# Three-stage transformer kernel: in the middle stage, probabilities turned by a transposing DMA per head and scores made in 64-row tiles

## The chip, the cores and the metric

The kernel runs on one core of a Trainium2 chip. The metric is the device time of one launch in microseconds; lower is better. Engines are named as the profile names them: PE is the matrix engine (PEld its weight loads), DVE the vector engine, ACT the scalar engine, POOL the GpSimd engine, SP the engine that only issues DMAs here. SBUF is the on-chip memory that all of them read; PSUM is the small accumulator memory that PE writes, in eight banks.

## The reference

`x` is [16, 112, 256] (16 batches of 112 tokens) and the context `ctx` is [16, 375, 256]. Three blocks follow one another: a cross-attention with 16 heads of 16 and a mixture of experts (first stage), a second cross-attention with 16 heads of 64 over context and tokens together (middle stage), and a mixture of 8 experts (last stage). The change touches the middle one:

```
heads, dim_head = (16, 64)
xn = layer_norm(x, g1, b1)                   # here x is the context, 375 rows
ln_lat = layer_norm(latents, g2, b2)         # 112 rows
q = ln_lat @ Wq
kv = jnp.concatenate([xn, ln_lat], axis=1) @ Wkv     # 375 + 112 = 487 rows
...
weight = jnp.einsum('bhld,bhnd->bhln', q * scale, k * scale)     # 112 x 487 a head
weight = jnp.where(full_mask[:, None, None, :], weight, neg)
weight = jax.nn.softmax(weight.astype(jnp.float32), axis=-1).astype(q.dtype)
out = jnp.einsum('bhln,bhnd->bhld', weight, v)
out = out.transpose(0, 2, 1, 3).reshape(b, l, heads * dim_head)
return out @ Wout
```

## The kernel before

Everything is computed in near float32 precision with 16-bit matmuls. A number is split into a high half (its float16 rounding) and a low half (what is left), and a product is three matmuls: high by high, high by low, low by high (`PASSES`).

The kernel has three stages, one after the other, each with its own program for each engine. The middle one is `phase_attention_large_heads`. Its names start with `b_` in the profile. It goes over the 16 batches. The bodies of batches 2 to 13 are a hardware loop of two batches an iteration (`run_batches`), the others are written out. A batch's body is 16 steps `s`, one a head (H = 16). There is no scheduler: each engine runs a list in the order of the code and waits on counters (`need`).

Work of a batch, by the steps of the body:

- **Projections** (`item`, 18 a batch, steps in `PSLOT`), for the batch after: 8 of K (128 x 487 results, 6 matmuls each), 2 of Q (24 matmuls of 112 columns), 8 of V (122 x 512 results, 6 matmuls; the 487 keys are cut in 4 blocks of KB1 = 122). Each result goes through one of two PSUM banks `ps_p`: ACT writes the high half, DVE the low half.
- **Stacking** (`stack`, on SP): a head has only 64 rows of K and Q, so DMAs put the high and low halves of K on top of one another (`k_stack`, 4 DMAs of 487 KB) and double those of Q (`q_dup`, 8 of 112 KB). This makes one head's three products two matmuls over 128 rows (`scores`).
- **Softmax**: `maxima` on DVE reads the scores from PSUM with the mask (`keep`) and writes `prob` and the row maxima; `exps` on ACT takes the exponential in place and the sums. `prob` is a ring of 4 heads (`RING`).
- **Transposes**: the product with V needs the probabilities with keys as rows. PE transposes `prob` in float32, 4 transposes a head, into a PSUM bank `ps_t` (`transposes`, two steps behind the scores). ACT copies out the high half (`phi`) and DVE the low half (`plo`), into `pT`, a ring of 2.
- **Values** (`values`, three steps behind the scores): 12 matmuls of 64 columns a head into one of two banks `ps_o`. `out_heads` on DVE divides by the sums once a batch.
- **Small work** (`XSLOT`, on a lent bank, `ps_x = ps_o[1]`): output projection, norms and the router for the batch before (`hitem`), transposes of the tokens two batches ahead (`nitem`). POOL splits tokens, makes the mask bias and rows for the experts, and splits the experts' weights for the last stage in chunks (`split_chunk`, 384 KB loads and stores).

Inside a step PE's list is: scores of head s, transposes of head s - 2, projections of the next batch, values of head s - 3, small work.

Of the kernel before, what the change touches and what calls it, by code (L numbers as in the profile page):

```python
# [16 lines left out]
ALU = mybir.AluOpType  # L17
# [8 lines left out]
B = 16  # L26
# [957 lines left out]
KB1, NB1 = 122, 4  # L984
# [3 lines left out]
def phase_attention_large_heads(nc, ctx_tok, mask, g_xattn, g_ffn, g1, b1, g2, b2, wr, br, consts, w_s,  # L988
# [6 lines left out]
    with ExitStack() as ctx:  # L995
# [32 lines left out]
        q_s = sb("q_s", [128, 2, IT, T], F16)  # L1028
        q_dup = [sb(f"q_dup{i}", [128, 2, H, T], F16) for i in range(2)]
        k_s = sb("k_s", [128, 2, IT, NK], F16)  # L1030
        k_stack = [sb(f"k_stack{i}", [128, H, NK], F16) for i in range(2)]
# [7 lines left out]
        pT = sb("pT", [128, 2, 2, NB1, 128], F16)  # L1039
# [67 lines left out]
        s_kstack = sem("kstack")  # L1107
        s_qdup = sem("qdup")
# [3 lines left out]
        s_tr = sem("tr")  # L1112
        s_phi = sem("phi")
        s_plo = sem("plo")
# [45 lines left out]
        XSLOT = {3: ("n", 0), 4: ("h", 0), 5: ("h", 1), 6: ("n", 1), 7: ("h", 2), 8: ("n", 2), 9: ("h", 3), 10: ("h", 4)}  # L1160

        def lent_before(s):

            n = [XSLOT[t][0] for t in XSLOT if t < s]
            return n.count("h"), n.count("n")
# [8 lines left out]
        def _(sp):  # L1174
            settled = (s_zero, 8)

            def load(c):
# [3 lines left out]
                sp.dma_start(x2_t[:, :], x2_dram[c]).then_inc(s_xload, 16)  # L1181
                need(sp, s_keep, 1, c, 0, settled)
                sp.dma_start(keep_u[:, :], mask[c].partition_broadcast(T)).then_inc(s_mload, 16)

            def stack(c, par):


                need_all(sp, settled, (s_ihi, PI, c, P_Q), (s_ifree, PI, c, P_Q), (s_score, H, c - 1, 1))
                for a in range(2):
                    for part in (HI, LO):  # L1190
                        src = k_s[64 * a:64 * a + 64, part, :, :]
                        rows = part if a == 0 else 1 - part
                        sp.dma_start(k_stack[par][64 * rows:64 * rows + 64, a::2, :], src).then_inc(s_kstack, 16)
                need_all(sp, settled, (s_ihi, PI, c, P_V), (s_ifree, PI, c, P_V))
                for a in range(2):
                    for rows in range(2):
                        for part in (HI, LO):
                            sp.dma_start(q_dup[par][64 * rows:64 * rows + 64, part, a::2, :],
                                         q_s[64 * a:64 * a + 64, part, :, :]).then_inc(s_qdup, 16)
# [5 lines left out]
            def store(c):  # L1205
                need(sp, s_hfree, HI_, c, H_X + 1, settled)
                sp.dma_start(acc_dram[bass.ds(c * T, T), :], x3[:, :]).then_inc(s_store, 16)

            def body(b, par):
                if not first(b):  # L1210
                    residual(b - 1)
                if ahead(b, 2):
                    load(b + 2)
                if ahead(b, 1):
                    stack(b + 1, 1 - par)
                if not first(b):
                    store(b - 1)

            load(0)
            load(1)  # L1220
            stack(0, 0)
            run_batches(sp, body)
            residual(B - 1)
# [4 lines left out]
        def _(pool):  # L1228
# [7 lines left out]
            pool.memset(prob[:, :, NK:NKP], 0.0).then_inc(s_zero, 1)  # L1236
# [24 lines left out]
            def split_tokens(c, par):  # L1261

                for k, cols in enumerate(TOK):
                    need_all(pool, settled, (s_nfree, NI, c, k + 1), *([(s_item, PI, c - 1, 0)] if k == 0 else []))
                    if first(c):
                        pool.wait_ge(s_thi, k + 1)
                    else:
                        pool.tensor_copy(tok_s[par][(slice(None), HI) + cols], tok_f[(slice(None),) + cols]).then_inc(s_tsplit, 1)
                        need(pool, s_tsplit, 6, c, 2 * k + 1)
                    pool.tensor_tensor(tok_s[par][(slice(None), LO) + cols], tok_f[(slice(None),) + cols],  # L1270
                                       tok_s[par][(slice(None), HI) + cols], ALU.subtract).then_inc(s_tsplit, 2 if first(c) else 1)
# [31 lines left out]
            def split_chunk(b, par, j, pair):  # L1303
# [5 lines left out]
                pool.tensor_tensor(wch_s[j][:, LO, :], wch_f[j][:, :], wch_s[j][:, HI, :], ALU.subtract).then_inc(s_wch, 1)  # L1309
                need(pool, s_wch, 4, b, 2 * j + 2, settled)  # L1310
# [17 lines left out]
            def choose(c):  # L1328
# [7 lines left out]
                pool.tensor_tensor(both[:, :], chosen[:, 0, :], chosen[:, 1, :], ALU.add).then_inc(s_chosen, 1)  # L1336
                need(pool, s_meta, 5, c, 0, settled)
# [8 lines left out]
            def send_rows(c):  # L1346
# [913 lines left out]
```

## Time and profile before

| | |
|---|---|
| time, median of 3 runs | 1531.97 us (1529.74 to 1535.42) |
| profiled execution, its own time | 1528.29 us |
| its span | 1526.3 us |
| PE busy | 1357.1 us (89%) |
| DVE busy | 1177.2 us (77%) |
| ACT busy | 954.2 us (63%) |
| POOL busy | 654.9 us (43%) |
| middle stage | from about 500 to 1315 us |
| mean granted TensorE clock | 0.953 |

Busy times count overlapping instructions of one engine once. Durations of single matmuls are longer than their share of the stream, since they are pipelined; the distance from one start to the next tells what one costs.

### The profile page before, as it was taken

What the parts mean: (1) busy time and instruction counts of PE and PEld (TensorE: products, weight loads), DVE (VectorE), ACT (ScalarE), POOL (GpSimd) and SP (SyncE); (2) the same over time, 40 slices, a digit from 0 to 9 for tenths busy, and PEclk for the clock granted to TensorE, in tenths of its full rate; (3) what the DMA queues carried; (4) which work ended last, traced back from release to release, by engine and by line L of the source; (5) the groups of instructions that cost most, each with busy time, mean ns of one, the idle gap of its engine ahead of it and who ended that gap; (6) DMA issues with size and microseconds to landing.
All of it is one profiled execution on the core that took longest, in us unless ns stands there. A gap on an engine that the chain in (4) does not pass through costs nothing. (4 is left out here: it accounts for less than half of the span.)

```text
span 1526.3 us, 45153 instructions
## 1 busy us (share of the span) xinstructions
PE 1357.1 (89%) x14276; PEld 1053.6 (69%) x14276; DVE 1177.2 (77%) x3350; ACT 954.2 (63%) x2456; POOL 654.9 (43%) x1044
## 2 busy tenths in 40 slices
PE   5999999999974799999999999999999997279995
PEld 3788888888751367776776677767766776278994
DVE  4899999999863388887887877878878787267772
ACT  4887888888951366665666665656656666045663
POOL 3544444444543234342543344334534424235654
PEclk8999999999976899999999999999999999589998
DMA  5333333333201666346653565447634671473323
GB/s 163 100 117 115 115 101 115 115 111 97 72 8 34 130 135 127 88 90 129 144 110 69 120 144 108 91 94 145 125 80 96 130 160 48 136 287 55 61 40 73
DMA packets 167807, 163.36 MB, mean 107 GB/s; under 512 B 81274, under 2 KB 155394, under 8 KB 164528
## 3 DMA queue, kind: packets, MB, share of 16 engines
q1 hardware_dynamic: 151440, 118.80, 34.2%
q0 software_dynamic: 13168, 35.80, 9.3%
q10 hardware_dynamic: 3024, 6.47, 1.5%
q8 instruction: 106, 1.74, 0.5%
q14 instruction: 69, 0.57, 0.1%
HBM read 64.48 MB, written 41.96 MB: 70 GB/s over the span
## 5 line engine op out<-in xcount | busy, mean ns | idle before, releaser
L1414 PE MATMUL b_ps_p<-b_tok_s,w_s 128*128 128x112 f16 (+1 forms) x1536 | 223.3, 300 | 11.3 <-DVE b_k_s L1698 6.6
L1709 DVE CUSTOM_DVE_ANT_0 b_prob<-b_ps_s,b_keep 112x487 f32<-112x487 f32 x256 | 167.9, 656 | 27.4 <-PE b_ps_s L1493 26.3
L1414 PE MATMUL b_ps_p<-w_s,b_tok_s 128*122 128x512 f16 x768 | 186.9, 379 | 0.0
L1605 ACT ACTIVATE b_prob<-b_prob,b_top 112x487 f32<-112x487 f32 x256 | 177.6, 694 | 10.5 <-DVE b_top L1709 10.3
L1414 PEld LDWEIGHTS b_ps_p<-b_tok_s,w_s 128*128 128x128 f16 x1536 | 117.5, 100 | 95.9 <-issue 17.9
L1611 ACT ACTIVATE b_pT<-b_ps_t 122x448 f16<-122x448 f32 x256 | 137.7, 538 | 72.1 <-PE b_ps_t L1501 69.6
L1493 PE MATMUL b_ps_s<-b_k_stack,b_q_dup 128*112 128x487 f16 x512 | 153.4, 382 | 25.6 <-issue 15.9
L1714 DVE TENSOR_TENSOR b_pT<-b_ps_t,b_pT 122x448 f16<-122x448 f32 x256 | 158.6, 619 | 6.9 <-ACT b_pT L1611 5.5
L701 ACT ACTIVATE a_prob<-a_prob,a_top 112x375 f32<-112x375 f32 x256 | 156.4, 611 | 4.4 <-DVE a_top L837 3.4
L837 DVE CUSTOM_DVE_ANT_0 a_prob<-a_ps_s,a_keep 112x375 f32<-112x375 f32 x256 | 138.2, 540 | 24.4 <-PE a_ps_s L593 21.8
L1521 PEld LDWEIGHTS b_ps_o<-b_v_s,b_pT 122*128 122x128 f16 x3072 | 122.5, 98 | 44.3 <-issue 6.6
L1501 PEld LDWEIGHTS b_ps_t<-b_const,b_prob 112*122 112x122 f32 x1024 | 121.6, 140 | 37.7 <-issue 1.5
L1584 ACT ACTIVATE b_k_s<-b_ps_p 128x487 f16<-128x487 f32 x128 | 73.9, 578 | 113.6 <-PE b_ps_p L1414 113.6
L842 DVE TENSOR_TENSOR a_pT<-a_ps_t,a_pT 125x336 f16<-125x336 f32 x256 | 128.2, 501 | 18.2 <-ACT a_pT L708 12.4
L1501 PE MATMUL b_ps_t<-b_const,b_prob 112*122 112x112 f32 x1024 | 142.2, 261 | 0.0
L1521 PE MATMUL b_ps_o<-b_v_s,b_pT 122*128 122x64 f16 x3072 | 131.8, 193 | 5.4 <-DVE b_pT L1714 3.4
L602 PE MATMUL a_ps_t<-a_const,a_prob 112*125 112x112 f32 x768 | 127.8, 275 | 9.0 <-ACT a_prob L701 7.1
L602 PEld LDWEIGHTS a_ps_t<-a_const,a_prob 112*125 112x125 f32 x768 | 113.9, 189 | 31.3 <-ACT a_prob L701 22.5
L1593 ACT ACTIVATE b_v_s<-b_ps_p 122x512 f16<-122x512 f32 x128 | 76.4, 597 | 93.8 <-PE b_ps_p L1414 93.8
L593 PE MATMUL a_ps_s<-a_k_stack,a_q_masked 128*112 128x375 f16 x512 | 126.4, 329 | 8.1 <-DMA a_q_masked<-a_q_s 7.6
L1414 PEld LDWEIGHTS b_ps_p<-w_s,b_tok_s 128*122 128x122 f16 x768 | 97.4, 134 | 45.2 <-DVE b_v_s L1705 2.5
L1705 DVE TENSOR_TENSOR b_v_s<-b_ps_p,b_v_s 122x512 f16<-122x512 f32 x128 | 88.5, 691 | 48.6 <-ACT b_v_s L1593 48.4
(259 smaller groups left out, 3062.1 us busy)
## 6 DMA issues: line engine op xcount, KB each, us to landing
b_k_stack<-b_k_s SPq DMA_DIRECT2D x64, 487.0 KB, 11.0
xs<-a_blank SPq DMA_DIRECT2D x14, 1032.0 KB, 4.0
b_q_dup<-b_q_s SPq DMA_DIRECT2D x128, 112.0 KB, 5.2
c_w_pool<-w_split SPq DMA_DIRECT2D x8, 1600.0 KB, 10.5
b_wch_f<-in_w_experts POOLq DMA_DIRECT2D x32, 384.0 KB, 11.8
w_split<-b_wch_s POOLq DMA_DIRECT2D x32, 384.0 KB, 7.2
a_ctx_f<-in_ctxT SPq DMA_DIRECT2D x16, 375.0 KB, 3.7
a_k_stack<-a_k_s SPq DMA_DIRECT2D x64, 93.8 KB, 2.8
```

The lines of the kernel that those rows point to most:

```text
L602: last = pe.transpose(ps_t[h % 2][0:KB0, j * T:(j + 1) * T], prob[:, h % RING, j * KB0:(j + 1) * KB0], ident[0:T, 0:T])
L701: act.activation(prob[:, h % RING, :], prob[:, h % RING, :], ACT.Exp, bias=top[:, h % RING:h % RING + 1], scale=-1.0, accum_out=sums[par][ ...
L837: dve.tensor_tensor_reduce(prob[:, h % RING, :], ps_s[h % 2][0:T, 0:C], keep[par][:, :], -SCALE0, 3e38, ALU.add, ALU.min, top[:, h % RING: ...
L842: dve.tensor_tensor(pT[0:KB0, h % RING, LO, :, 0:T], ps_t[h % 2][0:KB0, 0:NB0 * T].rearrange("p (j n) -> p j n", j=NB0), pT[0:KB0, h % RIN ...
L1414: last = pe.matmul(out, sta(a, k), mov(m, k), start=(k == 0 and n == 0), stop=(k == tiles - 1 and n == 2))
L1493: last = pe.matmul(ps_s[h % 2][0:T, 0:NK], q_dup[par][:, part, h, :], k_stack[par][:, h, :], start=(part == HI), stop=(part == LO))
L1501: last = pe.transpose(ps_t[h % 2][0:KB1, j * T:(j + 1) * T], prob[:, h % RING, j * KB1:(j + 1) * KB1], ident[0:T, 0:T])
L1521: last = pe.matmul(ps_o[h // 8][:, col:col + D1], pT[0:KB1, h % 2, a, j, :], v_s[par][0:KB1, m, j, h * D1:(h + 1) * D1], start=(h % 8 == 0 ...
L1605: act.activation(prob[:, h % RING, 0:NK], prob[:, h % RING, 0:NK], ACT.Exp, bias=top[:, h % RING:h % RING + 1], scale=-1.0, accum_out=sums ...
L1611: act.activation(pT[0:KB1, h % 2, HI, :, 0:T], ps_t[h % 2][0:KB1, 0:NB1 * T].rearrange("p (j n) -> p j n", j=NB1), ACT.Copy).then_inc(s_ph ...
L1709: dve.tensor_tensor_reduce(prob[:, h % RING, 0:NK], ps_s[h % 2][0:T, 0:NK], keep[par][:, :], -SCALE1, 3e38, ALU.add, ALU.min, top[:, h % R ...
L1714: dve.tensor_tensor(pT[0:KB1, h % 2, LO, :, 0:T], ps_t[h % 2][0:KB1, 0:NB1 * T].rearrange("p (j n) -> p j n", j=NB1), pT[0:KB1, h % 2, HI, ...
```

## The change

1. The 4 PE transposes a head, their PSUM banks `ps_t`, and `phi` and `plo` go. ACT now copies the high half of `prob` straight in SBUF, rows as they are, into `halves` (`high_half`). The low half is a subtraction SBUF to SBUF, on DVE for even heads and on POOL for odd ones (`low_half`). Then SP issues one transposing DMA a head (`turn`), which writes `pT`: 112 rows of 1024 float16 (both halves, 512 columns each) become 8 blocks of 128 x 112. `pT` and `halves` are rings of 4.
2. `stack`, `k_stack` and `q_dup` go. The scores of a pair of heads are 6 matmuls over 64 rows each, in turn on rows 0 to 63 and 64 to 127, straight from `k_s` and `q_s`, which are doubled. The scores have three PSUM banks in place of two, and small work has a bank of its own.
3. The key blocks are of 128, 128, 128 and 103 rows in place of 4 of 122 (`rows_of`).
4. The lists are laid out anew by steps: values come 5 steps behind the scores (`LAG`), scores of a pair at odd steps; `PSLOT` holds 2 projections in steps 0 and 1 and one in each of the other 14; `XSLOT` has other steps and also carries `ranks`; POOL's and SP's lists are spread over the steps; the division by the sums is done by halves.

```diff
-KB1, NB1 = 122, 4
+KB1, NB1 = 128, 4
+KLAST = NK - (NB1 - 1) * KB1
+LAG = 5
...
-        ps_s = [bank(f"ps_s{i}") for i in range(2)]
-        ps_t = [bank(f"ps_t{i}") for i in range(2)]
+        ps_s = [bank(f"ps_s{i}") for i in range(3)]
...
-        ps_x = ps_o[1]
+        ps_x = bank("ps_x")
...
-        for s, n in enumerate([2, 2, 2, 2, 1, 1, 0, 1, 1, 1, 1, 1, 1, 1, 1]):
+        for s, n in enumerate([2, 2] + [1] * 14):
...
+            def turn(b, h):
+
+                need_all(sp, settled, (s_lo[h % 2], H // 2, b, h // 2 + 1), (s_pv, H, b, h - RING + 1))
+                sp.dma_start(pT[:, h % RING, :, :, 0:T].rearrange("p s j n -> p (s j) n"),
+                             halves[:, h % RING, :, :].rearrange("p s n -> p (s n)"), transpose=True).then_inc(s_turned[h % RING], 16)
...
+            def scores(b, par, pair):
+
+                if pair == 0:
+                    need(pe, s_ihi, PI, b, P_V)
+                    need(pe, s_ifree, PI, b, P_V)
+                need(pe, s_max, H, b, max(2 * pair - 1, 0))
+                for n, (a, m) in enumerate(PASSES):
+                    for half in range(2):
+                        rows = slice(64 * half, 64 * half + 64)
+                        last = pe.matmul(ps_s[(2 * pair + half) % 3][0:T, 0:NK], q_s[par][rows, a, pair, :], k_s[par][rows, m, pair, :],
+                                         start=(n == 0), stop=(n == 2))
+                last.then_inc(s_score, 1)
...
+            def high_half(b, h):
+                need(act, s_exp, H, b, h + 1)
+                need(act, s_turned[h % RING], 16 * (H // RING), b, 16 * (h // RING))
+                act.activation(halves[:, h % RING, HI, 0:NK], prob[:, h % RING, 0:NK], ACT.Copy).then_inc(s_hi, 1)
...
+            def low_half(b, h):
+                need(dve, s_hi, H, b, h + 1)
+                dve.tensor_tensor(halves[:, h % RING, LO, 0:NK], prob[:, h % RING, 0:NK], halves[:, h % RING, HI, 0:NK],
+                                  ALU.subtract).then_inc(s_lo[0], 1)
...
             def body(b, par):
                 for s in range(H):
-                    scores(b, par, s)
-                    if not (first(b) and s < 2):
-                        c, _, h = behind(s, 2, b, par)
-                        transposes(c, h)
+                    if s == 0:
+                        scores(b, par, 0)
+                    if s % 2 == 1 and s < H - 1:
+                        scores(b, par, (s + 1) // 2)
                     if ahead(b, 1):
                         for k in PSLOT.get(s, []):
                             item(b + 1, 1 - par, k)
-                    if not (first(b) and s < 3):
-                        values(*behind(s, 3, b, par))
                     if s in XSLOT:
                         lend(b, s)
-                    if s == H - 1 and not first(b):
-                        ranks(b - 1)
+                    if not (first(b) and s < LAG):
+                        values(*behind(s, LAG, b, par))
```

On PE, late in the second batch, the list before reads (L1493 scores, L1501 transposes, L1414 a projection of V, L1521 values, L1449 small work):

```order
L1493 MATMUL b_ps_s<-b_k_stack,b_q_dup 112x487 x2
L1501 MATMUL b_ps_t<-b_const,b_prob 122x112 x4
L1414 MATMUL b_ps_p<-w_s,b_tok_s 122x512 x6
L1521 MATMUL b_ps_o<-b_v_s,b_pT 128x64 x12
L1449 MATMUL b_ps_o<-b_const,b_x_n 128x112 x2
```

and in the changed kernel, at the same place (L1537 scores of a pair, L1451 a projection of V, L1485 small work, L1552 values):

```order
L1537 MATMUL b_ps_s<-b_k_s,b_q_s 112x487 x6
L1451 MATMUL b_ps_p<-w_s,b_tok_s 128x512 x6
L1485 MATMUL b_ps_x<-b_const,b_x_n 128x112 x2
L1552 MATMUL b_ps_o<-b_v_s,b_pT 128x64 x12
L1451 MATMUL b_ps_p<-w_s,b_tok_s 128x512 x6
```

The transposes are gone, and the scores stand there every second step, as six matmuls instead of two.

On SP, the list of the second batch before is (L1203 the residual's load, L1180 to L1183 loads two batches ahead, L1207 the store):

```order
L1203 DMA b_x_res<-x 112x256
L1180 DMA b_ctx_t<-in_ctx 125x3x256
L1181 DMA b_x_t<-x 112x256
L1183 DMA b_keep_u<-in_mask 112x375
L1193 DMA b_k_stack<-b_k_s 64x8x487 x4
L1198 DMA b_q_dup<-b_q_s 64x8x112 x8
L1207 DMA acc<-b_x 112x256
```

and in the changed kernel:

```order
L1182 DMA b_ctx_t<-in_ctx 125x3x256
L1183 DMA b_x_t<-x 112x256
L1201 DMA_TRANSPOSE b_pT<-b_halves 128x8x112
L1192 DMA b_x_res<-x 112x256
L1201 DMA_TRANSPOSE b_pT<-b_halves 128x8x112 x5
L1188 DMA b_keep_u<-in_mask 112x375
L1201 DMA_TRANSPOSE b_pT<-b_halves 128x8x112 x6
L1196 DMA acc<-b_x 112x256
L1201 DMA_TRANSPOSE b_pT<-b_halves 128x8x112 x4
```

Twelve copies a batch went, and sixteen transposing DMAs came, one in each step, with the loads and the store between them.

On POOL, the list of the second batch before has its two weight chunks in a row (cast, low half, store, load of the next):

```order
L1307 CAST b_wch_s<-b_wch_f 128x768
L1309 TENSOR_TENSOR b_wch_s<-b_wch_f,b_wch_s 128x768
L1313 DMA w_split<-b_wch_s 128x2x768
L1301 DMA b_wch_f<-in_w_experts 128x768
L1307 CAST b_wch_s<-b_wch_f 128x768
```

and in the changed kernel (L1277 the low half of an odd head, L1260 the mask bias):

```order
L1314 CAST b_wch_s<-b_wch_f 128x768
L1316 TENSOR_TENSOR b_wch_s<-b_wch_f,b_wch_s 128x768
L1277 TENSOR_TENSOR b_halves<-b_prob,b_halves 112x487
L1260 TENSOR_SCALAR b_keep<-b_keep_u 112x375
L1323 DMA w_split<-b_wch_s 128x2x768
L1308 DMA b_wch_f<-in_w_experts 128x768
L1277 TENSOR_TENSOR b_halves<-b_prob,b_halves 112x487
L1314 CAST b_wch_s<-b_wch_f 128x768
```

The low half of an odd head stands behind whatever POOL does in the steps before it, a whole chunk's splitting above all.

## Rows read from the trace of the kernel before

**Rows 1.** Busy time of each engine by stretch, middle stage (last columns: clock, DMA share, GB/s).

```profile
core 0: us, PE busy (x) PEld busy (x) DVE busy (x) ACT busy (x) POOL busy (x), PEclk, DMA share, GB/s
800.00:900.00 100.00, 96.12 (x979) 70.59 (x978) 81.40 (x209) 62.15 (x142) 42.35 (x83) 0.98 0.55 114
```

**Rows 2.** The division by the sums (`out_heads`), two a batch: duration, first and last start.

```profile
L1725 DVE TENSOR_TENSOR b_o_n<-b_ps_o,b_rsum x32: 678/686/693, 584.0 to 1291.3; 112x512 f32<-112x512 f32 x32
```

**Rows 3.** Timeline of PE over one step (start us, us, what).

```profile
803.74 0.60 PE L1493 MATMUL b_ps_s<-b_k_stack,b_q_dup 128*112 128x487 f16 x2
804.18 0.55 PE L1501 MATMUL b_ps_t<-b_const,b_prob 112*122 112x112 f32 x4
804.56 1.46 PE L1414 MATMUL b_ps_p<-w_s,b_tok_s 128*122 128x512 f16 x6
805.86 0.52 PE L1521 MATMUL b_ps_o<-b_v_s,b_pT 122*128 122x64 f16 x12
806.21 0.60 PE L1493 MATMUL b_ps_s<-b_k_stack,b_q_dup 128*112 128x487 f16 x2
```

**Rows 4.** Timeline of PE where the loop starts anew, and the stretch's busy times.

```profile
716.27 1.05 PE L1493 MATMUL b_ps_s<-b_k_stack,b_q_dup 128*112 128x487 f16 x2 [2.98 <-issue]
...
716.00:718.00 2.00, 1.73 (x7) 1.33 (x8) 0.54 (x1) 0.00 (x0) 0.00 (x0) 0.53 0.21 24
```

**Rows 5.** The page's costliest groups: busy us, mean ns of one, idle before.

```profile
L1493 PE MATMUL b_ps_s<-b_k_stack,b_q_dup 128*112 128x487 f16 x512 | 153.4, 382 | 25.6 <-issue 15.9
L1611 ACT ACTIVATE b_pT<-b_ps_t 122x448 f16<-122x448 f32 x256 | 137.7, 538 | 72.1 <-PE b_ps_t L1501 69.6
L1714 DVE TENSOR_TENSOR b_pT<-b_ps_t,b_pT 122x448 f16<-122x448 f32 x256 | 158.6, 619 | 6.9 <-ACT b_pT L1611 5.5
L1584 ACT ACTIVATE b_k_s<-b_ps_p 128x487 f16<-128x487 f32 x128 | 73.9, 578 | 113.6 <-PE b_ps_p L1414 113.6
L1605 ACT ACTIVATE b_prob<-b_prob,b_top 112x487 f32<-112x487 f32 x256 | 177.6, 694 | 10.5 <-DVE b_top L1709 10.3
```

**Rows 6.** Groups of the middle stage: a low half on DVE (K) and one on POOL.

```profile
L1698 DVE TENSOR_TENSOR b_k_s<-b_ps_p,b_k_s 128x487 f16<-128x487 f32 x112 | 70.3, 658 | 26.0 <-ACT b_k_s L1584 26.0
L1309 POOL TENSOR_TENSOR b_wch_s<-b_wch_f,b_wch_s 128x768 f16<-128x768 f32 x30 | 49.4, 1645 | 4.2 <-POOL b_wch_s L1307 2.6
```

**Rows 7.** Timeline of SP's queue while a batch is stacked.

```profile
543.52 6.43 SPq L1193 DMA_DIRECT2D b_k_stack<-b_k_s  x4
550.05 11.76 SPq L1198 DMA_DIRECT2D b_q_dup<-b_q_s  x8
```

**Rows 8.** DMA queues, 540 to 560 us: share by tenths, then issues with KB and us to landing.

```profile
DMA  9590069695799999999999999999999999999999
b_k_stack<-b_k_s SPq DMA_DIRECT2D x4, 487.0 KB, 10.9
b_q_dup<-b_q_s SPq DMA_DIRECT2D x6, 112.0 KB, 5.3
b_wch_f<-in_w_experts POOLq DMA_DIRECT2D x1, 384.0 KB, 7.1
```

**Rows 9.** All 128 copies of Q: durations on SP's queue, us to landing (min/median/max).

```profile
L1198 SPq DMA_DIRECT2D b_q_dup<-b_q_s x128: 618/1774/4792, 509.3 to 1244.8; - x128
...
DMA to landing us min/median/max: 2.6/5.2/13.9
```

**Rows 10.** Timeline of PE at the first scores of the stage, and the clock there.

```profile
525.01 1.03 PE L1493 MATMUL b_ps_s<-b_k_stack,b_q_dup 128*112 128x487 f16 x2 [9.68 <-DMA b_q_dup<-b_q_s]
...
520.00:540.00 20.00, 12.34 (x55) 6.12 (x56) 10.93 (x26) 6.58 (x14) 6.50 (x9) 0.79 0.42 80
```

**Rows 11.** Timeline at the stage's end: last maxima, last values, first of the last stage.

```profile
1286.24 0.66 DVE L1709 CUSTOM_DVE_ANT_0 b_prob<-b_ps_s,b_keep 112x487 f32<-112x487 f32 x1
...
1290.12 0.51 PE L1521 MATMUL b_ps_o<-b_v_s,b_pT 122*128 122x64 f16 x12 [0.65 <-DVE b_pT L1714]
...
1315.18 0.17 PE L2035 MATMUL c_ps_a<-cum,ones 112*128 112x8 f16 x1 [7.07 <-PEq L995]
```

More of the change, by code:

```diff
@@ L1111, in phase_attention_large_heads @@
         s_exp = sem("exp")
-        s_tr = sem("tr")
-        s_phi = sem("phi")
-        s_plo = sem("plo")
+        s_hi = sem("hi")
+        s_lo = [sem("lo_even"), sem("lo_odd")]
+        s_turned = [sem(f"turned{i}") for i in range(RING)]
         s_pv = sem("pv")
@@ L1175, in _, with load_tokens @@
             settled = (s_zero, 8)
-            def load(c):
+            def load_tokens(c):
                 need(sp, s_norm, 2, c, 0, settled)
@@ L1181, in load, with load_mask @@
                 sp.dma_start(x2_t[:, :], x2_dram[c]).then_inc(s_xload, 16)
+            def load_mask(c):
                 need(sp, s_keep, 1, c, 0, settled)
                 sp.dma_start(keep_u[:, :], mask[c].partition_broadcast(T)).then_inc(s_mload, 16)
[L1185 to L1199, printed above, removed]
             def residual(c):
@@ L1497, in transposes @@
-            def transposes(b, h):
-                need(pe, s_exp, H, b, h + 1)
-                need(pe, s_plo, H, b, h - 1)
-                for j in range(NB1):
-                    last = pe.transpose(ps_t[h % 2][0:KB1, j * T:(j + 1) * T],
-                                        prob[:, h % RING, j * KB1:(j + 1) * KB1], ident[0:T, 0:T])
-                last.then_inc(s_tr, 1)
-            def values(b, par, h):
-                need(pe, s_phi, H, b, h + 1)
-                need(pe, s_plo, H, b, h + 1)
-                if h == 0:
-                    need(pe, s_oread, 2, b, 0)
+                elif kind == "n":
+                    nitem(b + 2, k)
+                else:
+                    ranks(b - 2)
@@ L1564, in _ @@
             run_batches(pe, body)
[L1565 to L1570 removed]
+            for h in range(H - LAG, H):
+                values(B - 1, 1, h)
+            need(pe, s_hfree, HI_, B - 1, 0)
+            ranks(B - 2)
+            need(pe, s_rank, 1, B - 1, 0)
             for k in range(HI_):
+                if k < H_O:
+                    need(pe, s_oread, 2, B - 1, k + 1)
                 need(pe, s_hfree, HI_, B - 1, k)
                 hitem(B - 1, k)
+            need(pe, s_hfree, HI_, B, 0)
             ranks(B - 1)
@@ L1619, in body @@
                 for s in range(H):
+                    if not (first(b) and s < 1):
+                        c, _, h = behind(s, 1, b, par)
+                        exps(c, 1 - par if s < 1 else par, h)
+                    if s == 0 and not first(b):
+                        for k in PSLOT[H - 1]:
+                            item(b, par, k)
                     if ahead(b, 1):
@@ L1653, in _ @@
             exps(B - 1, 1, H - 1)
-            phi(B - 1, H - 2)
-            phi(B - 1, H - 1)
+            high_half(B - 1, H - 1)
+            weigh(B - 2)
             for k in range(HI_):
@@ L1775, in ranks @@
                     dve.wait_ge(s_const2, NCONST2)
-                dve.tensor_tensor(rank[:, :], ps_p[0][0:T, 0:E], region[:, :], ALU.add).then_inc(s_rank, 1)
+                dve.tensor_tensor(rank[:, :], ps_x[0:T, 0:E], region[:, :], ALU.add).then_inc(s_rank, 1)
             def body(b, par):
                 for s in range(H):
+                    maxima(b, par, s)
+                    if s % 2 == 0 and not (first(b) and s < 2):
+                        c, _, h = behind(s, 2, b, par)
+                        low_half(c, h)
+                    if s == 0 and not first(b):
+                        for k in PSLOT[H - 1]:
+                            item(b, par, k)
                     if ahead(b, 1):
```

286 lines of the change are left out of this document (144 added, 142 removed).

## The prediction

> **What bounds the kernel now.** I read the busy times by stretch first: in the middle stage PE is busy 96 of 100 us, DVE 81, ACT 62, POOL 42, and the DMA engines 55% [rows 1]. The reader is to see that PE alone has no room, so this stage costs what PE's list costs. Next, the length of a batch: the divisions by the sums come twice a batch, the first starts at 584.0 us and the last, second of its pair, at 1291.3 [rows 2]. Less the 0.7 us between the two of a pair, that is 706.6 us for 15 batches, 47.1 us each. Then PE's timeline over one step, from start to start [rows 3]: two score matmuls 0.44 us, four transposes 0.38, six V matmuls 1.30, twelve value matmuls 0.35, together 2.47, with no idle time in it. The only large hole is where the loop starts anew: 2.98 us of issue, and a granted clock of 0.53 behind it, which is the 1.2 GHz level after PE had stood still [rows 4]. That comes once in two batches and belongs to the loop; I leave it in, unchanged.
>
> **The change part by part**, for a batch of 47.1 us.
>
> *The transposes go.* 16 heads by 0.38 us [rows 3]: 6.1 us off PE. Nothing lies over them, since PE is the full engine. PE: 41.0.
>
> *The scores.* Before, 16 by 0.44 = 7.0 us. Now a pair of heads takes six matmuls of 487 columns, one such being 0.22 us [rows 3]. The trace has no 64-row matmul. Below: the two halves of the array work at once, 3 by 0.22 = 0.66 us a pair. Above: they don't, 6 by 0.22 = 1.32. To either may come a drain when the array changes its shape and back. A bound for one drain is what a score matmul lasts over its share of the stream, 382 ns [rows 5] less 220, so 0.16, twice a pair 0.32. So a pair is between 0.66 and 1.64 us, a batch between 5.3 and 13.1. I take halves at once with the drain, 0.98 a pair, 7.8 a batch, since the two matmuls have different rows and banks and nothing of one depends on the other: 0.8 us more than before. PE: 41.8 (39.3 to 47.1 at the ends). Without the drains PE would be at 39.3 and the whole about 1413. The Trainium skill (TensorEngine Tiling (Array Packing), Key Properties) says that a change of the tiling mode drains the engine; no row here shows it, and by that rule the lower of the two times is out of reach.
>
> *Values and V.* Same counts and columns; blocks of 128 rows for 122 change no column. Zero; V's matmuls hide their loads.
>
> *ACT.* `phi` from PSUM is 538 ns; its successor reads 487 columns of SBUF, nearest the K copy's 578 [rows 5]. 16 by 0.04 = +0.6: 62.15% of 47.1 is 29.3, now 29.9 of 41.8.
>
> *DVE.* 16 by 0.62 goes [rows 5], 8 by 0.66 comes [rows 6]: 38.3 - 9.9 + 5.3 = 33.7 of 41.8, a share of 81%, the same as now. DVE stays behind PE.
>
> *POOL.* A low half there by the row of 768 columns, 1645 ns [rows 6]: 487 columns take 1.04, 8 by 1.04 = 8.3. 42.35% of 47.1 is 19.9; now 28.2 of 41.8. Queued behind a low half on POOL are the chunks, the mask bias and the rows, all due a batch later. The reverse matters: a low half waits up to 2.5 us for a chunk (its low half is 1.6 [rows 6], and I estimate half as much for its cast), and the turn of its head waits with it.
>
> *The DMA engines.* The trace has no transposing DMA. Before, 4 x 487 + 8 x 112 = 2844 KB a batch were stacked, in 18.3 us from 543.5 to 561.8 [rows 7] with the engines full [rows 8]: 155 KB/us, with a chunk's traffic beside it. Now 16 turns of 112 x 1024 x 2 bytes, 224 KB each. One turn costs all engines, if it moves like the K copies alone (1948 KB in 6.43 us), 0.74 us; like the Q copies alone, in pieces of 112 float16, 224 bytes (896 KB in 11.76, part of it K's backlog), 2.94 us. I take the two together, 1.44, since the turn's pieces lie near the small ones but the 2.94 holds the backlog. DMA: 55% of 47.1 = 25.9, less 18.3, plus 16 x 1.44 = 23.0, is 30.6 of 41.8. The Trainium skill (DMA: Bandwidth & Descriptors, Latency and other measured facts) gives 261 GB/s for a transposing DMA, an estimate of 0.88 us a turn, hence 21.7 of 41.8 for all traffic; the copies here went at 159 GB/s, and by neither figure do the engines bind.
>
> *Latency of a turn.* A Q copy of half the size lands after 2.6 us at the least, 5.2 in the median behind others of its queue [rows 9]; a K copy 10.9 and a chunk load 7.1 when the engines are full [rows 8]. For a turn alone I take 3.5, beside a chunk 5 to 6. The rings of 4 allow: high half 0.58, low 0.66 or 1.04, POOL's queue up to 2.5, the landing, all within 4 steps of 2.6 = 10.4 us. So landings up to about 6.3 us are hidden in the worst place, and 9 elsewhere. I give 0.4 us a batch for late ones and for the seam between batches, where scores wait for the last maxima: period 42.2.
>
> *Start of the stage.* PE waits 9.68 us for the first stacked Q and then has a mean clock of 0.79 over 20 us [rows 10]: half speed for 0.21 x 2 x 20 = 8.4 us, about 4 us lost. Scores now need only the projections: -13.
>
> *End.* From the last maxima to the last values it is 3.9 us now, 1286.24 to 1290.12 [rows 11]. With exponential 0.69 [rows 5], high 0.58, low 1.04, landing 3.5 and the hops between engines it is 7 to 10: +5. POOL's and DVE's small work of batch 14 now falls there too, under that landing.
>
> **Sum** against the profiled execution's 1528.3: (47.1 - 42.2) x 15 = 73.5 off, 13 off, 5 on: 1446.8. The median of the runs shown lies 3.7 over that execution, so about 1450.
>
> **The rivals.**
> - *Transposing DMAs are slow.* If a turn costs all engines 2.94 us, the DMA load is 7.6 + 47.0 = 54.6 us a batch: 15 x 7.5 = 113 more, less 8: 1637. It decides from (47.1 - 7.6) / 16 = 2.5 us a turn. For it: pieces of 224 bytes, and SP's queue gave 1.5 us to each of eight [rows 7]. Against: 618 ns at the least [rows 9], so issue isn't the limit. The same sign comes if SP needs over 2.9 us for each. 0.14.
> - *A turn's eight blocks go one after the other.* By rows: a block holds a quarter of a Q copy, whose least landing is 2.6 us [rows 9], so 0.65 a block and 5.2 a turn, 83 us a batch, or 1528 + 15 x 36 = 2070 and more. For it: PE turns a block in 0.095 us [rows 3], and nothing in the trace shows that the DMA engines turn at all. Against: copies spread over all engines and overlap [rows 8]. 0.03. The Trainium skill (VectorE: DVE Perf Modes, The three transpose paths) advises against the change in this sense: 1309 ns for a 128 x 128 by DMA, 390 by PE. By that page eight in a row would be 10.5 us; no run here shows it.
> - *Late landings.* The turn is fast enough but lands after 8 to 9 us beside chunks, so `high_half` waits for its ring slot and PE for `pT`, and holes of over 3 us lower the clock as at the loop's start [rows 4]. Period 44 to 46, say 45: 1532 - 32 - 8 = 1492. For it: chunk loads took 7.1 and K copies 10.9 [rows 8]. Against: the copies that filled the engines are gone. 0.17.
> - *The halves of the array don't run at once.* Six matmuls at full price and the drains: 47.1 again, so only the stage's start is won, about 1524, no change; without drains 44.6, about 1487. 0.09.
> - *Forecast*: PE stays the bound with turns hidden, 0.57, between 1413 and 1475.
>
> **How the numbers follow.** What a measurement tells from no change is about 0.5%, 7.7 us. Faster: 0.57, late landings 0.15, the array rival without drains 0.05, so 0.77. Same: 0.02 and 0.04, so 0.06. Slower: 0.14 and 0.03, so 0.17. The range starts at 1400, where 0.03 is left out, and goes to 1535, over the late landings and no change; the slow DMAs lie outside.
>
> **What would show it.** Right: divisions 42 us apart; scores of a pair starting within 0.2 us of one another and six of them within 1 us; DVE and PE at 80% and over 93%; turns landing within 6 us with no wait of PE or ACT for them; no hole at the first scores. Wrong: ACT's `high_half` or PE's values released by DMA; a DMA share over 90%; SP's turns back to back; the six score matmuls 0.22 us apart.

## The result, and the profile after

The changed kernel takes 1491.69 us (median of four) against 1531.86 beside it: ratio 0.9734, 95% interval 0.9713 to 0.9754. One of the four, 1890.42 us at a granted clock of 0.637, counts in that median but not in the ratio; the others lie between 1485.02 and 1494.09, with 1489.30 in the middle. It is faster by 2.7%, 40 us, where the forecast had 82.

The profiled execution has a time of 1494.09 us and a span of 1492.5, at a mean granted clock of 0.928 (0.953 before). Busy times by stretch, columns as in [rows 1]:

```profile
800.00:900.00 100.00, 88.45 (x903) 53.91 (x904) 77.01 (x202) 64.28 (x147) 62.64 (x96) 0.95 0.69 129
```

PE fell from 96% to 88%, and no other engine is above 77%: nothing is full. The gain of PE's list was made, and part of it stands as idle time. The group of the scores, with the starts of its first and last, tells how long the stage's work takes (before, then changed):

```profile
L1493 PE MATMUL b_ps_s<-b_k_stack,b_q_dup x512: 367/371/651, 525.0 to 1285.7; 128*112 128x487 f16 x171
```

```profile
L1537 PE MATMUL b_ps_s<-b_k_s,b_q_s x768: 363/367/653, 516.5 to 1240.6; 64*112 64x487 f16 x192
```

724.1 us from the first to the last, against 760.7. The batches of the loop show it more plainly. Between the first scores of batch 2 and those of batch 14 a batch takes 47.5 us (598.5 to 1168.8 us), and before 49.5 (618.2 to 1211.9): only 2.0 us went, where the forecast had 4.9. PE's timeline behind 836 us shows where it stands:

```profile
838.24 0.52 PE L1552 MATMUL b_ps_o<-b_v_s,b_pT 128*128 128x64 f16 x12
838.68 0.82 PE L1537 MATMUL b_ps_s<-b_k_s,b_q_s 64*112 64x487 f16 x6
841.63 2.64 PE L1451 MATMUL b_ps_p<-b_tok_s,w_s 128*128 128x487 f16 x12 [2.12 <-DVE b_v_s L1733]
844.11 0.52 PE L1552 MATMUL b_ps_o<-b_v_s,b_pT 128*128 128x64 f16 x12
844.55 0.83 PE L1537 MATMUL b_ps_s<-b_k_s,b_q_s 64*112 64x487 f16 x6
845.31 2.64 PE L1451 MATMUL b_ps_p<-b_tok_s,w_s 128*128 128x487 f16 x12
```

A batch begins at 838.68 with the scores of its first pair. The first projection of K should follow at once; it starts 2.95 us after the scores and waits for the low half of a V projection. That is the last projection of the batch before, and DVE has it behind two other things:

```profile
839.64 0.67 DVE L1738 CUSTOM_DVE_ANT_0 b_prob<-b_ps_s,b_keep 112x487 f32<-112x487 f32 x1 [0.55 <-PE b_ps_s L1537]
840.23 0.08 DVE L1738 DVE_READ_ACCUMULATOR2_ANT b_top<- 112x1 f32 x1
840.23 0.66 DVE L1743 TENSOR_TENSOR b_halves<-b_prob,b_halves 112x487 f16<-112x487 f32 x1
840.81 0.68 DVE L1733 TENSOR_TENSOR b_v_s<-b_ps_p,b_v_s 103x512 f16<-103x512 f32 x1
```

DVE even sits idle 0.55 us until the scores are there, takes the maxima, then a low half of probabilities, then the V low half. Where the loop starts anew, once in two batches, it is worse (PE, then DVE, then stretches of 2 us, in which the last three numbers are clock, DMA share and GB/s):

```profile
788.51 0.82 PE L1537 MATMUL b_ps_s<-b_k_s,b_q_s 64*112 64x487 f16 x6 [2.17 <-issue]
794.54 3.84 PE L1451 MATMUL b_ps_p<-b_tok_s,w_s 128*128 128x487 f16 x9 [5.21 <-DVE b_v_s L1733]
```

```profile
792.55 0.67 DVE L1738 CUSTOM_DVE_ANT_0 b_prob<-b_ps_s,b_keep 112x487 f32<-112x487 f32 x1 [5.88 <-POOL b_keep L1260]
```

```profile
791.00:793.00 2.00, 0.00 (x0) 0.00 (x0) 0.45 (x1) 0.00 (x0) 1.85 (x3) 0.50 0.30 82
...
795.00:797.00 2.00, 2.00 (x7) 0.72 (x6) 0.00 (x0) 0.00 (x0) 0.00 (x0) 0.50 0.85 207
...
799.00:801.00 2.00, 2.00 (x22) 1.10 (x21) 0.72 (x2) 1.36 (x3) 0.00 (x0) 0.88 0.00 0
```

PE stands 2.17 us, does six matmuls, stands 5.21 more, and then works on at 0.50, the 1.2 GHz level, until about 799. Before there was one hole of 2.98 us there [rows 4]. (The releaser named for DVE's 5.88 us is the mask bias, of which a batch's is made in the batch before; with the order of DVE changed, in the runs below, the same hole is named "issue". I read it as DVE's own restart.) The waits of PE from 600 to 1200 us, and one of ACT (total, times, longest):

```profile
PE b_ps_p L1451 <- DVE b_v_s L1733: 39.5, 13, 5.2
PE b_ps_s L1537 <- issue: 14.1, 5, 5.0
PE b_ps_x L1451 <- DVE b_tok_f L1715: 6.8, 12, 0.7
PE b_ps_o L1552 <- DMA b_pT<-b_halves: 4.8, 7, 1.1
ACT b_halves L1636 <- DMA b_pT<-b_halves: 20.2, 17, 2.5
```

The wait for turned probabilities is the smallest of PE's four. ACT's wait for a landing, one of the forecast's signs of being wrong, did come up: `high_half` waits 17 times for a free part of `halves`. But ACT is busy only 64% of the time, and PE's own wait for landings is the 4.8 us. The turns themselves (durations on SP's queue in ns, us to landing):

```profile
L1201 SPq DMA_TRANSPOSE b_pT<-b_halves x256: 1221/1229/2932, 523.1 to 1249.4; - x128
...
DMA to landing us min/median/max: 2.9/3.3/8.8
```

### The profile page after: what moved, and what is told of

Same layout as the page of the kernel before. It is cut to its first block and busy times, and to the rows that moved or that the text cites. A ratio compares the mean times of both kernels' runs of the same rounds, so it can differ in the third digit from the quotient of the medians.

```text
span 1492.5 us, 43700 instructions
## 1 busy us (share of the span) xinstructions
PE 1278.8 (86%) x13508; PEld 918.0 (62%) x13508; DVE 1126.8 (75%) x3238; ACT 953.7 (64%) x2456; POOL 822.4 (55%) x1172
## 5 line engine op out<-in xcount | busy, mean ns | idle before, releaser
L1451 PE MATMUL b_ps_p<-b_tok_s,w_s 128*128 128x112 f16 (+1 forms) x1536 | 238.6, 308 | 46.5 <-DVE b_v_s L1733 42.8
L1277 POOL TENSOR_TENSOR b_halves<-b_prob,b_halves 112x487 f16<-112x487 f32 x128 | 147.9, 1156 | 140.5 <-ACT b_halves L1636 140.3
L1451 PEld LDWEIGHTS b_ps_p<-b_tok_s,w_s 128*128 128x128 f16 x1536 | 112.0, 101 | 156.6 <-issue 82.6
L1451 PE MATMUL b_ps_p<-w_s,b_tok_s 128*128 128x512 f16 (+1 forms) x768 | 187.7, 380 | 0.0
L1636 ACT ACTIVATE b_halves<-b_prob 112x487 f16<-112x487 f32 x256 | 155.3, 607 | 32.6 <-DMA b_pT<-b_halves 32.0
L1552 PEld LDWEIGHTS b_ps_o<-b_v_s,b_pT 128*128 128x128 f16 (+1 forms) x3072 | 124.5, 100 | 40.8 <-DMA b_pT<-b_halves 18.1
L1552 PE MATMUL b_ps_o<-b_v_s,b_pT 128*128 128x64 f16 (+1 forms) x3072 | 135.2, 195 | 13.2 <-DMA b_pT<-b_halves 13.1
L1725 DVE TENSOR_TENSOR b_k_s<-b_ps_p,b_k_s 128x487 f16<-128x487 f32 x128 | 84.9, 663 | 72.1 <-ACT b_k_s L1610 71.9
L1618 ACT ACTIVATE b_v_s<-b_ps_p 128x512 f16<-128x512 f32 (+1 forms) x128 | 75.7, 592 | 72.9 <-PE b_ps_p L1451 70.9
L708 ACT ACTIVATE a_pT<-a_ps_t 125x336 f16<-125x336 f32 x256 | 115.1, 449 | 10.5 <-PE a_ps_t L602 9.8
L1537 PE MATMUL b_ps_s<-b_k_s,b_q_s 64*112 64x487 f16 x768 | 108.9, 390 | 15.0 <-issue 14.1
L1451 PEld LDWEIGHTS b_ps_p<-w_s,b_tok_s 128*128 128x128 f16 (+1 forms) x768 | 70.9, 105 | 77.2 <-issue 9.7
L1733 DVE TENSOR_TENSOR b_v_s<-b_ps_p,b_v_s 128x512 f16<-128x512 f32 (+1 forms) x128 | 87.9, 687 | 28.5 <-ACT b_v_s L1618 27.4
```

The source lines that it names most:

```text
L708: act.activation(pT[0:KB0, h % RING, HI, :, 0:T], ps_t[h % 2][0:KB0, 0:NB0 * T].rearrange("p (j n) -> p j n", j=NB0), ACT.Copy).then_inc(s ...
L1277: pool.tensor_tensor(halves[:, h % RING, LO, 0:NK], prob[:, h % RING, 0:NK], halves[:, h % RING, HI, 0:NK], ALU.subtract).then_inc(s_lo[1], 1)
L1451: last = pe.matmul(out, sta(a, k), mov(m, k), start=(k == 0 and n == 0), stop=(k == tiles - 1 and n == 2))
L1552: last = pe.matmul(ps_o[h // 8][:, col:col + D1], pT[0:k, h % RING, a, j, :], v_s[par][0:k, m, j, h * D1:(h + 1) * D1], start=(h % 8 == 0 ...
L1636: act.activation(halves[:, h % RING, HI, 0:NK], prob[:, h % RING, 0:NK], ACT.Copy).then_inc(s_hi, 1)
```

## The experiments

Every ratio is against the kernel before on the same chip, with its interval; I turn differences into us with 1531. **Theory A** is the seam between batches, ordinary and at the loop's restart. Its rivals: late landings (B), a longer list on PE (C). "Scores" is the span from the first to the last score matmul; "batch" is the mean of batches 2 to 13, from first scores to first scores; clock and DMA share are those of 600 to 1100 us. The changed kernel's last scores stand two steps earlier in their batch, so between the two kernels the column "batch" is the fair one.

| run | time, us | ratio | scores, us | batch, us | clock | DMA share |
|---|---|---|---|---|---|---|
| before | 1531.9 | 1 | 760.7 | 49.5 | 0.98 | 0.54 |
| before, no loop | 1501.7 | 0.9816 (0.979 to 0.9842) | 736.2 | 47.2 | 1.00 | 0.57 |
| changed | 1491.7 | 0.9734 (0.9713 to 0.9754) | 724.1 | 47.5 | 0.94 | 0.69 |
| exact wait | 1460.2 | 0.955 (0.9524 to 0.9576) | 696.5 | 45.6 | 0.98 | 0.73 |
| DVE first | 1457.4 | 0.952 (0.9494 to 0.9545) | 690.7 | 45.4 | 0.97 | 0.74 |
| no loop | 1454.1 | 0.9513 (0.9493 to 0.9534) | 684.2 | 44.5 | 0.98 | 0.74 |
| exact wait, DVE first | 1441.7 | 0.9442 (0.9405 to 0.9479) | 670.6 | 44.0 | 0.98 | 0.78 |
| all three | 1410.3 | 0.9227 (0.9209 to 0.9246) | 641.2 | 41.5 | 1.00 | 0.80 |

**The exact wait.** The bank of a projection is free when the item two before it is read. For k = 0 the line waits for one more than that, all 18 items:

```diff
-                need(pe, s_ifree, PI, c, max(k - 1, 0))
+                need(pe, s_ifree, PI, c, k - 1)
```

> Edit: the changed kernel, but a batch's first K projection waits on PE only for the projection item that used its PSUM bank before (item 17 of 18 counts as still running), instead of for all 18 items of the batch before. Theory A (seams between batches): PE stands 2.1 to 2.5 us at every batch's step 0 for DVE's low half of the last V projection; with the exact wait the first projection starts behind the scores and only the second still waits. The wait of PE for that V low half (39.5 us over the 13 batches of 600 to 1200 us) falls to about 15, the time by 12 to 25 us, to about 1470 to 1480. Theory B (late landings of the turned probabilities): the time stays at 1492 within 3 us, since the holes only move to the values.

Measured: 28 us less. PE's wait for the V low half, 600 to 1200 us, was 39.5 and is now:

```profile
PE b_ps_p L1451 <- DVE b_v_s L1733: 23.8, 12, 4.3
```

23.8 us is more than the 15 expected, the gain in time a little more too: 16 us of wait and, I infer from the mean clock of 0.98 for 0.94, the rest at the restarts, where PE now does a projection between the two holes. B is out as the main cause.

**DVE first.** The last V low half moved ahead of the low half of the probabilities, and of the maxima:

```diff
                 for s in range(H):
+                    if s == 0 and not first(b):
+                        for k in PSLOT[H - 1]:
+                            item(b, par, k)
                     maxima(b, par, s)
...
-                    if s == 0 and not first(b):
-                        for k in PSLOT[H - 1]:
-                            item(b, par, k)
```

> Edit: the changed kernel, only DVE's order at a batch's step 0: the low half of the last V projection ahead of the first low half of the probabilities. The wait for all 18 items stays. Theory A: the seam's hole of 2.49 us is 1.4 us of DVE's other work (low half 0.66, and the place behind the maxima) and the rest the chain projection, ACT, DVE; so it falls to about 1.1 to 1.8, 0.7 to 1.4 us a batch for 14, and the stretch at half clock behind the loop's restart falls from 10.2 towards 3.4 us: 1460 to 1482. Rival (the order is nothing without the exact wait): 1490.

Measured: 33 us less, just more than expected. An ordinary seam on PE's timeline:

```profile
729.21 0.82 PE L1537 MATMUL b_ps_s<-b_k_s,b_q_s 64*112 64x487 f16 x6
730.42 2.64 PE L1451 MATMUL b_ps_p<-b_tok_s,w_s 128*128 128x487 f16 x12 [0.38 <-DVE b_v_s L1733]
```

From scores to projection it is 1.21 us in place of 2.95. Either edit alone gives most of what both give (45 us, below): they shorten one hole.

**No loop.** `run_batches` and `run_pairs` replaced on all five engines by

```python
for b in range(B):
    body(b, b % 2)
```

(On POOL the body gets `b // 2` as well.)

> Edit: the changed kernel with the middle stage's 16 batches written out on all five engines, no hardware loop. Theory A (seams): each start of an iteration, six in all, costs the changed kernel a hole of 5 to 8 us on PE and DVE and then 10 us at half the clock, about 12 us together, so 6 x 12 = 72 us at the most; of that the wait at the seam itself stays (2.5 us each), so 45 to 60 us go: 1432 to 1447, near the forecast of 1450. Theory B (late landings): the loop's start costs what it cost before, 3 us and 1.7 us of slow clock: -28 us or less, about 1465, and the waits of ACT and PE for landings stay. Theory C (PE's list itself is longer than forecast): less than 15 us go.

Measured: 34 us less. More than B's price, less than mine: a seam's hole stays in every batch (30.4 us, 13 times, the longest 2.3), and what a restart costs is 34 / 6 = 5.6 us, not 8 to 10. Why it is less than its holes and slow clock suggested, no run shows.

**The control: before without a loop.**

> Edit: the kernel before with the middle stage's 16 batches written out, no hardware loop: the control for the run of the changed kernel without a loop, which gained 38 us. Theory D (the changed kernel's restart of the loop is worse than before's): before, each of the six starts of an iteration cost a hole of about 3 us and 3.4 us at half the clock, 4.7 us, so about 6 x 4 = 20 to 28 us go: 1500 to 1508. Rival (the loop costs both kernels the same): 38 us go, 1490. If the first holds, 10 to 18 us of the missing gain are the loop's, which the forecast left in unchanged.

Measured: 28 us less. The loop cost the kernel before 4.7 us a restart and the changed one 5.6. So the restart alone did not eat the gain: it is 6 us of the missing 42, about what the intervals leave open.

**All three edits.**

> Edit: the changed kernel with no hardware loop, the exact wait for the bank and DVE's last V low half ahead of the first maxima. Theory A: both kinds of seam gone, so the period is PE's list, 41 us or a bit below: 1494 - 72 - 25 = 1397 at the least, 1400 to 1425 likely; mean granted clock in the middle stage back at 0.98. Theory B: PE is released by DMAs instead (values, high halves), 1440 to 1460.

Measured: 1410.3. Between 600 and 1100 us PE is full again, at the 2.4 GHz level throughout:

```profile
800.00:900.00 100.00, 98.70 (x1042) 60.81 (x1041) 90.58 (x240) 75.47 (x173) 76.46 (x116) 1.00 0.84 155
```

PE's wait for DMAs over 600 to 1150 us is 7.5 us in it (6 times), so turns are not what binds even then. C is out too: a batch takes 41.5 us, against 47.2 in the kernel before without its loop, 5.7 us less.

**Exact wait and DVE first, loop kept.**

> Edit: the changed kernel with its hardware loop, the exact wait for the bank and DVE's last V low half ahead of the first maxima. The wait at the ordinary seam is gone (2.5 us in each batch, as in the run without a loop), the loop's restart stays: the run without a loop and with both edits took 1410, and a restart costs a hole of 6 us and slow clock of a few us, 7 to 8 us each with six of them: 1450 to 1458. If DVE's order matters only together with the written-out loop: 1460, as with the exact wait alone.

Measured: 1441.7, 45 us less than the changed kernel, better than I expected by 8 to 16 us. An ordinary seam has no wait in it any more: the scores start at 725.36, the projection at 726.12. The seam cost 45 us of the time, and 3.5 us of every batch (47.5 to 44.0). What is left at a restart (PE, then DVE):

```profile
768.90 1.46 PE L1537 MATMUL b_ps_s<-b_k_s,b_q_s 64*112 64x487 f16 x6 [2.21 <-issue]
770.29 2.42 PE L1451 MATMUL b_ps_p<-b_tok_s,w_s 128*128 128x487 f16 x6
773.43 1.41 PE L1451 MATMUL b_ps_p<-b_tok_s,w_s 128*128 128x487 f16 x6 [0.72 <-DVE b_v_s L1733]
```

```profile
772.68 0.69 DVE L1733 TENSOR_TENSOR b_v_s<-b_ps_p,b_v_s 103x512 f16<-103x512 f32 x1 [5.64 <-issue]
```

DVE still stands 5.64 us there, but PE now has a projection to do meanwhile: its second hole is 0.72 us in place of 5.21.

**Scores by head.** The six matmuls of a pair in another order, all three of the first head and then all three of the second:

```diff
-                for n, (a, m) in enumerate(PASSES):
-                    for half in range(2):
+                for half in range(2):
+                    for n, (a, m) in enumerate(PASSES):
```

> Edit: the changed kernel, but the six score matmuls of a pair come head by head (three on rows 0 to 63, then three on rows 64 to 127), not in turn. If the halves of the array work at once only when neighbouring matmuls are on different halves, a pair goes from 3 to 5 units of 0.2 us: +0.4 us a pair, +3.3 us a batch, +45 to 52 us in all where PE is the bound: about 1540. If PE has room (theory B, landings bind), +10 us or less. If concurrency is not what makes the scores cheap, no change. The starts of the six matmuls: three 0.2 us apart, one at 7 ns, two 0.2 apart.

Measured: 1488.7, ratio 0.9741 (0.9721 to 0.9762), no change. The question was whether concurrency needs neighbours on different halves. Counting the score matmuls in flight in two stretches of one such group, 0.20 us each:

```profile
841.79:841.99 0.20, 0.20 (x2) 1.00 0.89 184
842.04:842.24 0.20, 0.20 (x4) 1.00 0.00 0
```

Two from the start, as in the changed kernel, and the group lasts 0.83 us in both. So "no change" came true, but not with its reason: matmuls do run two at once, in either order. The records don't say on which rows a matmul ran. That each of the two is on another half is my inference; in this order the two starts of a pair lie 10 ns apart, in the changed kernel 3.

**Loads behind the restart.** SP issues the loads of tokens and residual, 599 KB, just ahead of the restart. In two kernels they come in steps 3 and 4, behind the turns, with DVE's statistics two steps and POOL's root one step later (not shown in the diff):

```diff
-                    if s == 0 and ahead(b, 2):
-                        load_tokens(b + 2)
-                    if s == 1 and not first(b):
-                        residual(b - 1)
...
                         turn(c, h)
+                    if s == 3 and ahead(b, 2):
+                        load_tokens(b + 2)
+                    if s == 4 and not first(b):
+                        residual(b - 1)
```

> Edit: as the kernel with the exact wait and DVE's low half first, loop kept; and SP issues the loads of tokens and residual (375 + 112 + 112 KB) in steps 3 and 4, behind the turns of the restart, instead of ahead of it; DVE's statistics two steps later, POOL's reciprocal root one. Theory E (these loads fill the DMA engines just when the loop's start needs them for its instructions, and that is why DVE stands 5.7 us): DVE's hole at the restart falls from 5.7 to about 3 us as before the change, 2.5 us and some slow clock each, 15 to 30 us in all against the same kernel with early loads. Rival (the turns themselves, or the length of DVE's code, make the hole): within 5 us of it, hole unchanged; or slower by 5 to 10 where statistics come late.

> Edit: the changed kernel with only the loads moved behind the restart, as in the run above. Theory E: 10 to 25 us less than 1492, and the stretch at half clock after the restart shorter than 10.2 us. Rival: within 5 us of 1492.

Measured: with the seam mended 1450.4, ratio 0.9497 (0.9467 to 0.9527), 8 us slower than with early loads, with intervals that just overlap; on the changed kernel 1496.2, ratio 0.9785 (0.9748 to 0.9821), at best no change. Yet the hole did what Theory E said. DVE's waits from 600 to 1120 us with the seam mended, early loads and then late loads:

```profile
DVE b_v_s L1733 <- issue: 28.0, 5, 5.8
```

```profile
DVE b_v_s L1733 <- issue: 16.2, 5, 3.5
DVE b_bns L1694 <- DMA b_ctx_t<-in_ctx: 11.8, 7, 1.9
```

5.6 us a restart became 3.2, and 12 us of it came back as a new wait: DVE's statistics now wait for the tokens. These loads lengthen the hole, by a mechanism that is not shown; as a way to a faster kernel moving them falls.

**Plain copies for turns.** The kernel with exact wait and DVE first, in which a turn copies the rows without turning them (so the values are made from unturned probabilities):

```diff
-                sp.dma_start(pT[:, h % RING, :, :, 0:T].rearrange("p s j n -> p (s j) n"),
-                             halves[:, h % RING, :, :].rearrange("p s n -> p (s n)"), transpose=True)
+                sp.dma_start(pT[0:T, h % RING, :, :, :].rearrange("p s j n -> p (s j n)"),
+                             halves[:, h % RING, :, :].rearrange("p s n -> p (s n)"))
```

> Edit: the kernel with its loop, the exact wait and DVE's low half first (1442 us), in which each turn is a plain copy of the same 224 KB, rows left as rows, in pieces of 2048 bytes; the probabilities are then not turned, so this computes something else, and only the time counts. Theory F (the turns' small pieces fill the DMA engines): DMA share falls from 0.77 to about 0.45, the landing of a copy is 2 us and not 3.4, the waits of ACT and PE for landings (21 and 4 us) go, and DVE's hole at the restart of the loop (5.6 us) falls to 3 to 4: 1425 to 1432. Rival (turns are hidden and the hole is from the loads of 600 KB alone): within 5 us of 1442.

Measured: 1434.3, ratio 0.9378 (0.9351 to 0.9406), but the scores' span is 671.4 us, the same as with turns (670.6). That is the sum of two opposite things. From 600 to 1120 us PE waits 4.4 us for turned probabilities with turns and not at all with copies, and 11.2 us at the loop's restarts with turns and 18.7 with copies. So late landings show as some 0.4 us of PE's waits a batch with turns. The profiled executions differ by 3.7 us, of which 2.5 is the earlier start of the first scores. The copies lasted 512 ns on SP's queue and landed after 2.6 us (turns: 1244 and 3.4). DVE's hole grew from 5.6 to 6.8 us a restart, with less DMA traffic. So Theory F falls: it is not the turns' small pieces that lengthen it.

**Every turn twice.**

```diff
+                sp.dma_start(spare[:, h % RING, :, 0:T], halves[:, h % RING, :, :].rearrange("p s n -> p (s n)"),
+                             transpose=True).then_inc(s_turned[h % RING], 16)
```

> Edit: the same kernel as that of the run above, but with every turn issued twice, the first into a tile that nothing reads. It prices a turn. By the forecast's term a turn takes all DMA engines for 1.44 us and the other traffic 7.6 us a batch: 7.6 + 32 x 1.44 = 54 us against a batch of 41.8, so the DMA engines become the bound and the time is 1442 + 15 x 12 = 1620 or more, DMA share over 95%. Rival (a turn's share is mostly latency, or the engines overlap better): SP's queue with 32 x 1.23 = 39 us a batch is not yet the bound, and the time stays under 1480.

Measured: 1654.7, ratio 1.0816 (1.0786 to 1.0845), as expected (1620 or more). The DMA engines are the bound, and PE's wait for turned probabilities is 72.7 us from 600 to 1120 us, in place of 4.4. Windows 600 to 1100 us of the three, turned once, copied, turned twice:

```profile
600.00:1100.00 500.00, 470.28 (x4935) 289.67 (x4934) 420.08 (x1090) 348.27 (x796) 356.13 (x551) 0.98 0.78 144
```

```profile
600.00:1100.00 500.00, 471.59 (x4919) 290.40 (x4919) 417.72 (x1086) 347.19 (x791) 355.02 (x549) 0.97 0.48 144
```

```profile
600.00:1100.00 500.00, 401.01 (x3836) 236.47 (x3834) 329.88 (x852) 272.75 (x618) 275.01 (x429) 0.91 1.02 178
```

The last three numbers are clock, DMA share and GB/s; I read a share above 1 as packets' times that overlap a little. A batch takes 44.0, 44.2 and 56.3 us in these (batches 2 to 13); times the share that is 34.3, 21.2 and 57.4 us of all DMA engines. Sixteen more turns add 23.1, 1.44 us each; the same bytes as a plain copy cost 0.82 less, 0.62.

## Why the prediction was right in sign and wrong in size

By spans of the profiled executions, the forecast was 73.5 + 13 - 5 = 81.5 us off, and 33.8 went.

- **The sign, and the work removed: right.** PE was the bound and its list became shorter. Without loops and with the seam mended a batch is 5.7 us shorter than before, where I had 6.1 off and 0.8 on, 5.3. The 6.1 for the transposes is not to be separated from the rest by a run.
- **The length of a batch was misread.** [rows 2] go from the division of batch 0, which stands in the list of batch 1, to that of batch 15, which follows its own values at once. So 47.1 is too short: from scores to scores it is 49.5 in the loop. In the sum it cancels, since both periods carry it.
- **The scores: the branch was right, the size too high.** From 844.55 to 845.31 a pair takes 0.76 us in the list, and the values ahead of it take 0.44 (844.11 to 844.55) in place of 0.35, so 0.85 in all, where I took 0.98 with two drains; before it was 2 x 0.44. That is 1.0 us a batch less than I had. Two matmuls run at once; the rival that they don't (0.09), six at full price, is out. Three streams of 487 columns at 0.21 each (twelve K matmuls, 841.63 to 844.11, are 2.48) make 0.62, so 0.14 there and 0.09 at the values are left as what the drains could be. The Trainium skill (TensorEngine Tiling (Array Packing), Key Properties) has such a drain at each change of mode; the trace is consistent with there being one, at less than the 0.32 a pair that I had given.
- **The DMA engines: right, the second decimal by luck.** 1.44 us a turn was forecast and 1.44 measured. The forecast was the joint rate of two kinds of copies, between 0.74 and 2.94, chosen without a row of a turn; that it fits so closely is chance, and the 0.88 that stands beside it was too low. 30.6 us of traffic a batch was forecast, and 0.69 of 47.5 us, 32.8, measured. A turn lands after 3.3 us in the median (forecast 3.5 alone). The rival of slow turns was not the case; what it says of so high a price is borne out: with 2 x 1.44 us a head the time is 1654.7, where the rival had 1637 for 2.94. The rival of eight blocks in series is out: the Trainium skill (VectorE: DVE Perf Modes, The three transpose paths) has 1309 ns for a 128 x 128 by DMA, and here eight blocks of 128 x 112 together land in 3.3.
- **The step that failed** is the sentence "I give 0.4 us a batch for late ones and for the seam between batches, where scores wait for the last maxima". I had looked at the scores' wait. It is the first projection that waits, for the last projection of the batch before. Two lines make it together: `PSLOT` now has an item in step 15, where before the last was in step 14, so at the seam it is still on its way through ACT and DVE; and the wait for k = 0, which was there before, asks for all 18 items. Before, with that wait but an empty step 15, the list of PE's waits has none for a V low half. The term was 0.4 us a batch; the seam measured 3.5. Mending both lines gives 45 us back and lands at 1441.7, near the 1450 forecast for a list without such a hole. That is partly luck: the pairs of scores cost 1.0 us a batch less than in the sum, 15 us in all, and the end cost more.
- **"I leave it in, unchanged"** failed as a part of this. The restart alone is not much dearer (written out, the batches save 5.6 us a restart, and 4.7 before), but the seam's wait falls into it: PE stops twice in a row, 2.17 and 5.21 us, and stays at half the clock until about 799. Before it stopped once, for 2.98 us.
- **Late landings** were given 0.17 and 1492 us. The number was met, by chance, and the mechanism was not: PE waits 4.8 us in 600 for turned probabilities, the hole of the seam goes without a faster landing, and plain copies, which land 0.8 us earlier, leave the scores' span where it was. Those 4.8 us are some 0.4 a batch, what I had given for late landings and seam together.
- **The ends.** The first scores start 8.5 us earlier (525.01 to 516.51). My 13 also had about 4 us of slow clock behind the wait; that part falls into the first batch, which takes 37.8 us in place of 45.0, with a clock of 1.00 from 520 to 540 us in place of 0.79. So both parts of the 13 are there; how much of the second is the clock's and how much the shorter list's is not separated. The last score matmul is 37.3 us before the last stage's first matmul, in place of 29.5; I had +5 for the end and it is +7.8, of which the last pair's place, two steps earlier, is a part. The last stage took 214.6 us for 211.1, which no run here explains. The scores' span gave 36.6, where I had 73.5, and the four parts make up the whole: 8.5 + 36.6 - 7.8 - 3.5 = 33.8.

## What to carry to other kernels

When a change puts work into a slot that was empty (here the last step of a batch), look up every wait written for the batch boundary and ask what it really needs; an over-wait by one item cost nothing here as long as the slot was empty. Price a seam by the chain that ends last across it, for each engine's first instruction of the new batch, not for the one that the change is about. And a hole next to another one costs more than its length: behind the two the clock was at 0.50 until about 799, behind the one that was left (768.90) it was back at 1.00 by 773.

The best version here is the changed kernel with the exact wait, DVE's V low half first and the batches written out: 1410.3 us, 7.7% under the kernel before. With the loop kept it is 1441.7.

## What the runs showed of the hardware

- Six 64-row matmuls of 487 columns, three on each half of the rows, run two at once even where three of one half stand ahead of three of the other in the list: two in flight from the first moment, 0.83 us for six in either order. Which two run together the records don't say.
- A transposing DMA of 112 x 1024 float16 within SBUF costs all DMA engines 1.44 us, SP's queue 1.23 us and 3.3 us to landing; a plain copy of the same bytes 0.62, 0.51 and 2.6.
- DVE stands 5.6 us at a loop's restart, 3.2 with 599 KB of loads moved away from it and 6.8 with plain copies in place of turns. The first suggests that these loads lengthen it, the second that less traffic alone doesn't shorten it. What it waits for is not shown; this stays open.
